# One gather moved ahead of six stores, and the row moments of two batches moved a third of a stream earlier

## The reference, cut to what matters

```
xn     = layernorm(x)
q      = xn @ Wq;   latent = (xn @ Wk + xn @ Wv) @ Wdown
k, v   = latent @ Wup_k, latent @ Wup_v            # 16 heads of 8 columns
scores = (q k^T * scale) * exp(-c |i - j|)          # 1024 x 1024 a head and batch
x      = x + (softmax(scores) @ v) @ Wo
x      = x + fp8grid(layernorm(x) / s_in) @ fp8grid(W8 / s_k) * s_in * s_k + bias
```

## Time and profile before

| what | value |
|---|---|
| runs | 575.83 us median, 573.82 to 578.02 |
| profiled execution | 575.56 us, of which the trace spans 573.8 |
| ACT busy | 486.2 us, 85% of the span |
| PE busy | 496.8 us, 87% of the span |
| DVE busy | 315.1 us, 55% of the span |
| POOL busy | 178.3 us, 31% of the span |
| idle time of ACT ahead of its exponentials | 36.1 us, 23.2 of it put down to DVE L891 |
| granted TensorE clock, mean | 0.961 of full speed |
| first and last exponential of the four streams | within 24 to 540 us; after 540 the last unit's tail |

### The profile page before, as it was taken

One profiled execution on the slowest core, in us unless ns is written; L12 is line 12 of the kernel. 1 busy time (PEld: TensorE's weight loads), 2 busy tenths in 40 slices (PEclk: granted clock), 3 DMA queues, 4 the chain that ended last, 5 costly groups with the idle time before them and its releaser, 6 DMA issues.

```text
span 573.8 us, 9316 instructions
## 1 busy us (share of the span) xinstructions
PE 496.8 (87%) x3451; PEld 114.6 (20%) x3451; DVE 315.1 (55%) x768; ACT 486.2 (85%) x523; POOL 178.3 (31%) x123
## 2 busy tenths in 40 slices
PE   2787779989998999989998999989999999999620
PEld 1321111122111221222121212222122111121110
DVE  5376345345557665546557565556565564456344
ACT  1455769989999999979999999989999999999600
POOL 2499401877100206694100216691100010001001
PEclk9988989999999999989999999999999999999955
DMA  6364899637797400655997001557977000100000
GB/s 202 110 221 156 247 194 213 182 125 265 187 221 161 115 8 6 222 188 177 247 198 153 25 6 39 191 192 221 253 150 163 9 7 6 43 5 6 24 3 21
DMA packets 46096, 74.06 MB, mean 129 GB/s; under 512 B 6176, under 2 KB 27360, under 8 KB 45920
## 3 DMA queue, kind: packets, MB, share of 16 engines
q1 hardware_dynamic: 44512, 72.70, 47.1%
q10 hardware_dynamic: 1536, 0.73, 0.5%
HBM read 35.40 MB, written 35.65 MB: 124 GB/s over the span
## 4 chain that ended last, share of the span: by engine, by line
PE 44%; ACT 26%; POOL 8%; issue 8%; DVE 6%; DMA 4%; SPq 3%; ACTq 0%; POOLq 0%; DVEq 0%
ACT probs L548 25%; PE ps L702 22%; PE ps L689 13%; POOL sq L446 2%; POOL sq L448 2%; POOL parts L450 2%; PE ps L619 2%; PE ps L624 2%; PE ps L587 2%; DMA Qs<-qp_dram 2%; DVE ps L891 1%; DMA qp_dram<-parts 1%; PE ps L591 1%; SPq L357 1%; POOL parts L447 1%
## 5 line engine op out<-in xcount | busy, mean ns | idle before, releaser
L548 ACT ACTIVATE probs<-ps 128x1024 f32<-128x1024 f32 x512 | 480.4, 1060 | 36.1 <-DVE ps L891 23.2
L702 PE MATMUL ps<-probs,V 128*9 128x512 f32 x2048 | 270.8, 601 | 3.8 <-DVE V L994 1.1
L891 DVE TENSOR_TENSOR ps<-ps,consts 128x256 f32<-128x256 f32 (+1 forms) x256 | 143.5, 565 | 173.2 <-PE ps L689 156.1
L689 PE MATMUL ps<-Qs,Ks 64*128 64x512 bf16 x960 | 176.5, 387 | 23.9 <-ACT probs L548 11.0
L689 PEld LDWEIGHTS ps<-Qs,Ks 64*128 64x128 bf16 x960 | 42.4, 93 | 289.4 <-ACT probs L548 266.4
L475 POOL TENSOR_TENSOR xs<-xs,magic 128x512 f32<-128x512 f32 x8 | 10.2, 1274 | 232.6 <-DVE magic L949 232.6
L702 PEld LDWEIGHTS ps<-probs,V 128*9 128x9 f32 x2048 | 31.3, 88 | 83.8 <-issue 59.9
L897 DVE COPY pv_out<-ps 105x512 f32<-105x512 f32 x32 | 22.1, 690 | 29.2 <-PE ps L702 29.2
L439 POOL TENSOR_TENSOR X<-X,mv 128x512 f32<-128x512 f32 x7 | 7.3, 1043 | 80.2 <-DVEq L1050 71.3
L448 POOL TENSOR_TENSOR sq<-sq,parts 128x768 f32<-128x768 f32 (+1 forms) x16 | 31.6, 1974 | 1.3
L446 POOL TENSOR_TENSOR sq<-kT,decay 128x768 f32<-128x768 f32 x8 | 15.6, 1945 | 52.9 <-DVE kT L986 42.5
(11 more groups left out here) (102 smaller groups left out, 264.4 us busy)
## 6 DMA issues: line engine op xcount, KB each, us to landing
Qs<-qp_dram SPq DMA_DIRECT2D x32, 512.0 KB, 9.0
qp_dram<-parts SPq DMA_DIRECT2D x16, 768.0 KB, 4.6
Ks<-kp_dram SPq DMA_DIRECT2D x32, 384.0 KB, 7.4
kp_dram<-parts SPq DMA_DIRECT2D x16, 576.0 KB, 4.3
qp_dram<-parts SPq DMA_DIRECT2D x8, 512.0 KB, 6.0
kp_dram<-parts SPq DMA_DIRECT2D x8, 384.0 KB, 4.8
X<-L_attn_x SPq DMA_DIRECT2D x4, 512.0 KB, 7.0
kt_dram<-kT SPq DMA_DIRECT2D x4, 512.0 KB, 9.8
```

The costliest lines, as they stand in the source:

```text
L548: nc.scalar.activation(probs[:, quad % RING, 2 * jp:2 * jp + 2, :].rearrange("p j n -> p (j n)"), ps_all[:, bank * CH:(bank + 2) * CH], AC ...
L689: last = nc.tensor.matmul(bank, Ks[half, g, jp, key_cols(v, kc)], Qs[half, g, jp, v, qh * CH:(qh + 1) * CH], start=True, stop=True)
L702: last = nc.tensor.matmul(pv[32 * j:32 * j + VW, :], V[:, unit // 2 * NB + kc, HG * j + g, :], probs[:, quad % RING, j, :], start=i == 0, ...
L891: nc.vector.tensor_tensor(own, own, factors, ALU.mult).then_inc(fixed, 1)
```

## The change

Two edits. In SP's program the gather of a first unit's last group stands ahead of the stores of the next batch's key parts, where it stood behind them. In DVE's program the row statistics of the third and fourth batch (b = 2 and 3) are worked in the stream before the one in which they were: statistics of four tiles in quad 51, of the other four in quad 55, moments in quad 58, the twelve steps in quads 60 to 63, where they stood in quads 3 to 11 of the next stream. Those of the second batch keep their places. The moments now also wait for the normalised rows of the batch before, because the same buffers are used.

```diff
                         for first in range(F32_GROUPS):
                             stage(0, first)
-                    if qh == 0 and g == 3 and b < B - 1:
-                        store_parts(b + 1, 0)
                     if qh == 1 and g == 0 and b < B - 1:
                         store_parts(b + 1, 1)
                     if g < G - 1 or unit < UNITS - 1:
                         gather(group)
+                    if qh == 0 and g == 3 and b < B - 1:
+                        store_parts(b + 1, 0)
                     if qh == 1 and b < B - 1:
...
             def prepare_rows(b, at):
 
-                if at == 3:
+
+                if b == 1:
+                    tiles, moments = {3: range(NB)}, 5
+                    places = {5: range(5), 6: (5, 6), 8: (7, 8), 10: (9, 10), 11: (11,)}
+                else:
+                    tiles, moments = {-13: range(4), -9: range(4, NB)}, -6
+                    places = {-4: (0, 1, 2), -3: (3, 4), -2: (5, 6, 7), -1: range(8, 12)}
+                if at in tiles:
                     dve.wait_ge(x_in[b], 16)
-                    tile_stats(b, range(NB))
-                elif at == 5:
+                    tile_stats(b, tiles[at])
+                if at == moments:
+                    dve.wait_ge(xn_ready[1], b)
                     tile_moments(range(NB))
-                for i in {5: range(5), 6: (5, 6), 8: (7, 8), 10: (9, 10), 11: (11,)}.get(at, ()):
+                for i in places.get(at, ()):
                     inverse_std_step(i, mv, rs)
-                if at == 11:
-                    settle()
-                    dve.sem_inc(stats_ready, 1)
+                    if i == 11:
+                        settle()
+                        dve.sem_inc(stats_ready, 1)
...
                 if b < B - 1:
                     prepare_rows(b + 1, quad % STREAM)
+                if b < B - 2:
+                    prepare_rows(b + 2, quad % STREAM - STREAM)
```

## The result

The changed kernel took 580.58 us (median of 18 runs, 578.6 to 582.7) against 575.92 for the kernel before (18 runs): a ratio of 1.0077, 95% interval 1.0058 to 1.0095. It is slower, by 4.4 us by the ratio and 4.7 by the medians. The forecast was 577.6 us against a profiled 575.56, so 2.0 (2.3 from the two parts, less 0.3 for the clock). Its profiled execution took 580.55 us, with a span of 578.8.

A forecast was written before the change was run, and what follows sets the result against it. ACT's exponentials, 480.4 us busy in unbroken chains, were taken as the bound, so only gaps count. Gather 3.9 us slower, moments 1.6 faster, clock 0.3 off: 577.6 us against a profiled 575.56, own range 575 to 580.5.

The forecast's parts named there:

- held twice: Rival: in quad 47 the steps wait for both squares, 3.0 us lost in each stream, 583.0 us in all; chance 0.15.
- The gather is early enough: Quad 39: moved ahead, the gather starts at 110.7 and lands about 117.5, removing a 1.67 us wait three times.
- POOL waits for the landing of the key stores: First query split: it waits for the first-sign key stores to land at about 121.4 to 121.7, 3.9 us later.
- The widening is shut out: Quad 39: L908 waits for POOL's L446, price between 0 and 1.5 us, upper taken; gather gains 0.6 us a stream.
- The steps of quad 47: L796 and L800 wait for POOL, L798 slips between; slot 96 is 1.2, 1.5, 1.2 us later, gather's gain included.
- The steps of quad 48 cost nothing: Quad 48: steps 3 and 4 meet POOL's L471, with 1 us to spare before DVE's next copy: no cost.
- The moments give 1.6: Gap of 1.01 us ahead of slot 136 closes twice, 2.0 us; 0.2 lost twice ahead of slot 124: 1.6 faster.
- The clock: Second stream's slow clock, about 1.3 us of extra gaps, can vanish or move to a new gap; 0.3 us taken off.
- SP's lateness costs nothing: Stages and later gathers behind the key stores on SP shift similarly, with more than 3 us in hand: no cost.

The follow-up runs named there:

- the late squares: The changed kernel with POOL's two squares put behind the grid of the first unit: 585.86 us, ratio 1.0149 to the kernel before.
- POOL late in the kernel before: The kernel before, with only POOL's query splits of batches two to four held until slot 78 has been through ACT: 584.51 us, ratio 1.0131.

## Why the prediction was right

The direction, the places and the mechanism came out as forecast; the size was under half, 2.0 us where 4.4 were measured. In the profiles the first stream lost 2.0 us (0.4 forecast), the third 1.7 (1.2), and the second nothing (0.7), as its slow clock of before was gone. The 580.58 lies at the upper edge of the forecast's own range of 575 to 580.5. The rival "held twice" (583) is not what happened, as L798 went through the pause in all three streams. Step by step:

- **The gather is early enough.** Right: issued from 112.21 (110.7 forecast, in a stream that is 1.5 us later here), and L902 in quad 39 waits for no DMA.
- **POOL waits for the landing of the key stores.** Right in kind (L446 released by the DMA of the parts, in all three streams). The size was short: 6.5, 5.9 and 6.0 us from the first store's issue to the split, where the prediction had 5.3 to 5.6. The 0.6 us by which it was longer in the first stream put POOL behind the widening there.
- **The widening is shut out.** Right in streams two and three, where the price was more than I took: 2.0 us above its usual 0.69, and no gain of the gather is left (1.67 and 1.68 us of gap, against 1.76 and 1.69). In the first stream POOL came 0.4 us later than DVE, the clash fell away, and the stretch up to slot 95 gained the 1.44 us that PE's idle time of 1.64 had set as the bound. Of the two bounds of the prediction, the whole instruction and the 0.25 us seen before, the Trainium skill (SBUF — State Buffer, "Who interferes with whom") has the first; the 2.69 us agrees with it.
- **The steps of quad 47.** Right to a tenth in the third stream (1.72 us lost, 1.8 forecast), and for the reason given: L796 waits for the last split, L798 goes through the pause, L800 waits for L470. In the second the size is near (1.70 lost, with the gain of the moments in it; 1.3 forecast for the two together), but POOL is not 1 us further on: the rows are those of the third stream. In the first L800 waits for L450 instead, as POOL is 1.9 us further back.
- **The steps of quad 48 cost nothing.** Wrong in the first stream. This is the term that was mis-sized: since POOL ran to 146.4, L802 and L804 were both held, 1.48 and 1.82 us, and ACT had gaps of 1.01 and 1.46 ahead of slots 100 and 101. The stretch from 95 to 136 lost 3.4 us, where my working had 1.0. The clock was granted at 0.87 in the ten us from 140 on; how much of the gap of 1.46 is its doing stays open (with the gather alone the same gap is 0.98, also behind a slow clock). In streams two and three L802 was held too, for 1.27 us, and cost ACT 0.16 us at most, as forecast.
- **The moments give 1.6.** Right within what the runs tell: 2.7 us by themselves (interval 0.7 to 4.8). ACT's timelines put it at 1.9, 0.97 for each of the two gaps of 1.01, since the five steps in quads 60 and 61 cost no gap, where 0.2 was allowed for them twice.
- **The clock.** The second stream's slow stretch didn't return (granted 1.00 from 250 to 260), which is most of the 1.70 us gained from slot 185 to 223. The profile of the moments alone has no slow stretch there either, behind the same gap, so this gain isn't put down to the change. Two other stretches are slow instead, each behind a new gap ahead of slot 96: 140 to 150 (0.87) and 270 to 280 (0.83). The prediction named this possibility and took 0.3 off for its opposite.
- **SP's lateness costs nothing.** True of this kernel's time, but not for the reason given. I had checked the next unit's first gather and the staging's deadline, not the last gather, which queues in the DMA engines behind the late stages. L902 in quad 71 waited three times, where I had said it would wait for no DMA outside the last unit; the late squares showed what that wait costs once nothing else is slow.

## What to carry to other kernels

A wait that stands behind stores in a queue is cheap to remove, but ask who waits for the stores: here they freed buffers for an engine two steps away, and its whole later run moved. Two engines that exclude each other are timed against each other as well as by their own dependencies; when an order is changed, lay the two timelines side by side again. And a late transfer may be held by the bytes ahead of it in the DMA engines and not by its issue: where that was so, small DMAs that someone waits for went ahead of large ones that nobody needed yet, and it paid.

## What the runs showed of the hardware

The exclusion holds down to the smallest instructions: a step on 128x4 numbers with 0.17 us of work took 2.00 us beside one POOL instruction, and in these rows the next one slips in where POOL pauses (0.18 us ahead of a new split, under 0.1 inside one). The integer shift L798, which I had counted among those that never wait, took 1.82 us when it found POOL at work (POOL late in the kernel before). Order decides here: 0.4 us ahead of POOL's instruction the widening took 0.69 us, and 0.2 us behind it 2.69. The last of eight DMAs of 2 and 16 KB landed 7 us after its issue behind stages that kept the DMA share at 1.04, and 1.4 us after it where the share was 0.06 to 0.08 (kernel before, 120 to 124 us).
